# Layer 0 attention in a four-layer kernel: one head at a time, or four heads and blocks of 32 queries

## The reference

```python
q, k, v = heads of (layernorm(x) @ w_qkv.T)          # 16 heads of 8
content = einsum('bhid,bhjd->bhij', q, k)
rel_scores = qE taken at clip(j - i, -64, 64) + 64   # qE = q @ rel_emb.T
scores = (content + rel_scores) / sqrt(8)
scores = where((j > i) | (i - j >= 32), -inf, scores)
out = softmax(scores) @ v
x = x + out @ w_out.T
```

## Time and profile before

| | us |
|---|---|
| median of 3 runs | 3664.6 |
| the profiled execution | 3654.07 |
| its span | 3652.2 |
| stage 3 (preparation of the first attention unit) | 56.0 |
| stage 4 | 100.6 |
| stage 5 | 88.1 |
| stage 6 | 87.3 |
| stage 7 | 113.3 |
| stage 8 (last finish of the attention) | 37.3 |

### The profile page before, as it was taken

How to read it: one execution, slowest core, us unless ns; L and a number is a source line. 1 busy time by engine, 2 the same in 40 slices (tenths; PEclk the granted TensorE clock), 3 DMA queues, 4 the chain that set the end, 5 groups by cost and what they waited for, 6 DMA issues and landing times. The chain is left out here.

```text
span 3652.2 us, 63921 instructions
## 1 busy us (share of the span) xinstructions
PE 2966.9 (81%) x23249; PEld 1869.6 (51%) x23249; DVE 2404.7 (66%) x6402; ACT 1929.6 (53%) x5094; POOL 899.9 (25%) x875
## 2 busy tenths in 40 slices
PE   5868888878987558899787787889887889889875
PEld 3545544544443434456675587656554333556553
DVE  4667765677777456786456543868776677777752
ACT  2356775245553225555246633656664677667652
POOL 1000000011133331111213211635451112444430
PEclk7879988689988779999898988989998899999987
DMA  3423432000000000003660056300000000001010
GB/s 121 166 76 100 110 102 67 1 1 1 1 1 1 1 1 1 1 1 103 222 210 6 12 194 212 100 20 23 14 23 4 1 1 1 21 14 24 13 29 9
DMA packets 132658, 183.41 MB, mean 50 GB/s; under 512 B 48501, under 2 KB 108021, under 8 KB 130682
## 3 DMA queue, kind: packets, MB, share of 16 engines
q1 hardware_dynamic: 129818, 174.14, 15.3%
q0 software_dynamic: 2048, 4.20, 0.3%
q10 hardware_dynamic: 480, 0.98, 0.1%
HBM read 131.90 MB, written 30.61 MB: 44 GB/s over the span
## 5 line engine op out<-in xcount | busy, mean ns | idle before, releaser
L1051 DVE TENSOR_REDUCE nm<-ps 128x1 f32<-128x512 f32 (+4 forms) x832 | 443.3, 564 | 111.8 <-PE ps L972 63.7
L1094 ACT ACTIVATE core<-ps 128x512 f32<-128x512 f32 (+3 forms) x832 | 377.0, 510 | 131.0 <-PE ps L1003 91.7
L274 POOL TENSOR_TENSOR rstd<-ve,weights 128x4 f32<-128x4 f32 x80 | 80.9, 1011 | 1290.4 <-DVE ve L251 1289.9
L969 PE MATMUL ps<-hand 128*128 128x128 bf16 (+3 forms) x1024 | 302.4, 335 | 57.5 <-DVE nm L1051 31.2
L427 ACT COPY hand<-ps 64x512 bf16<-64x512 bf16 x448 | 259.6, 580 | 139.4 <-PE ps L459 100.7
L1000 PE MATMUL ps<-hand 128*128 128x512 bf16 (+3 forms) x1024 | 273.5, 309 | 18.6 <-ACT hand L427 9.4
L1890 POOL TENSOR_TENSOR pre<-pre,sin 128x512 f32<-128x512 f32 x128 | 221.9, 1754 | 241.3 <-ACT pre L1859 225.5
L2006 ACT ACTIVATE core<-ps,nm 128x128 f32<-128x128 f32 x512 | 181.8, 374 | 124.4 <-DVE nm L2021 123.7
L1659 PE MATMUL ps<-hand 128*128 128x128 f32 x1408 | 199.7, 302 | 38.5 <-DMA hand<-in_experts 38.5
L1895 POOL TENSOR_TENSOR ss<-ss,weights 128x16 f32<-128x16 f32 x64 | 194.2, 3035 | 117.4 <-DVE ss L1910 115.9
L1818 PE MATMUL ps<-weights,pre 128*128 128x512 f32 x384 | 207.1, 637 | 17.4 <-ACT pre L1862 17.3
(11 more groups left out here) (331 smaller groups left out, 7542.6 us busy)
## 6 DMA issues: line engine op xcount, KB each, us to landing
hand<-in_experts SPq DMA_DIRECT2D x88, 836.0 KB, 4.9
core<-shear SPq DMA_DIRECT2D x64, 512.0 KB, 3.8
shear<-post SPq DMA_DIRECT2D x64, 256.0 KB
hand<-hand SPq DMA_DIRECT2D x16, 512.0 KB, 4.4
hand<-hand SPq DMA_DIRECT2D x16, 384.0 KB, 5.6
pre<-sorted_in SPq DMA_DIRECT2D x8, 704.0 KB, 4.7
sorted_out<-core SPq DMA_DIRECT2D x88, 64.0 KB, 2.3
core<-in_stream SPq DMA_DIRECT2D x2, 2048.0 KB, 7.8
```

The costliest lines, as they stand in the source:

```text
L969: ins = nc.tensor.matmul(b[:, n * P:n * P + nk], q[:, qt * P:(qt + 1) * P], k[:, lo:lo + nk], start=kind != BLOCK32, stop=True, skip_group ...
L1051: nc.vector.tensor_reduce(nm_of(h, qts), src, AX.X, ALU.max, negate=True).then_inc(negmax, 1)
L1094: nc.scalar.activation(prob8[:, i % PROBS, 0:L - q0], m.ps[:, RING[at % NR], 0:L - q0], ACT.Exp).then_inc(ring_out, 1)
```

## The change

The core is written anew for layer 0; `attend_near` is gone. A unit is now a group of four heads and half of the tokens: 8 units instead of 64. The 512 queries are cut into 16 blocks of 32, each with 64 keys, its own 32 and the 32 before. Four heads lie on the four quarters of the partitions and eight blocks side by side, so a unit's scores are one full bank, 128 x 512. Per unit there are 32 score matmuls (32 columns of weights, 64 moving), three VectorE instructions over 128 x 512 (add, minimum of each 64, subtract), one exp of 128 x 512 without a sum, four transposes, one copy, and 32 fp32 matmuls with the values (64 rows, 32 columns of weights, 32 moving). The row sum comes from a column of ones that already stands in the values, and the division moves to the finish. Half of the blocks have keys that begin at row 32 or 96 of a tile; for them `Vs`, a copy of the values shifted by 32 tokens, is made by two DMAs at the end of the preparation. The relative scores come by 64 DMAs of 32 KB in place of 16 of 512 KB. `far` is a constant that masks the keys before the first block. The finish becomes `divide` (16 transposes, 4 reciprocals, 4 products) and `out_project` (4 transposes, a copy, 4 matmuls, an addition), helpers that other layers use, with a plain output weight of 128 columns where 512 were. The order strings of stages 3 to 8 are new.

```diff
-    [("ip_T", NI), ("pv", 4 * DV), ("l0_qkv", 3 * D), ("l0_out", 4 * D),
+    [("ip_T", NI), ("pv", 4 * DV), ("l0_qkv", 3 * D), ("l0_out", D),
...
-def attend_near(nc, m, note, a, heads, rows_of, value_of, place_of, sheared):
...
+    def vector(dve):
+        yield 0.0
+        dve.wait_ge(*stacks_turned)
+        nc.vector.memset(a.Vs[0:32, 0, :], 0.0).then_inc(none_set, 1)
+
     def sync(sp):
+
+        yield 0.1
+        sp.wait_ge(*stacks_turned)
+        sp.dma_start(a.Vs[32:128, :, :], a.V[0:96, :, :]).then_inc(moved, 16)
+        sp.dma_start(a.Vs[0:32, 1:NT, :], a.V[96:128, 0:NT - 1, :]).then_inc(moved, 16)
...
+    units = [(g, half) for g in range(4) for half in range(2)]
+    U = len(units)
+    BQ, BK = 32, 64
+    NPR, NTS, NREL = 3, 3, 2
+    TURN, WEIGH = 2, 3
+    S, PT, O = (0, 1), (2, 3), (4, 5)
...
+        for t in (2 * half, 2 * half + 1):
+            for odd in range(2):
+                for r in range(2):
+                    yield 4 * t + 2 * r + odd, (t % 2) * 256 + odd * 128 + r * 64, (a.V if odd else a.Vs)[:, t, :], 64 * r
...
+        for g in range(4):
+            yield max(0.0, 2.0 * (g - NREL + 1) + 0.6)
+            if g >= NREL:
+                sp.wait_ge(added, 2 * (g - NREL + 1))
+            for j in range(4):
+                h = 4 * g + j
+                for odd in range(2):
...
+                    for r in range(2):
...
+                        sp.dma_start(dst[:, :, odd, r], src).then_inc(rel_in[g % NREL], 16)
...
+            if i >= 2:
+                pe.wait_ge(added, i - 1)
+            if half == 0:
+                nc.tensor.matmul(out[:, 0:BK], m.identb, m.far, start=True, stop=True)
+            for n, at, _, _ in blocks(half):
+                for j in range(4):
...
+                    ins = nc.tensor.matmul(out[BQ * j:BQ * (j + 1), at:at + BK], q[:, BQ * n:BQ * (n + 1)], keys,
+                                           start=n > 0, stop=True, skip_group_check=True)
...
+            pe.wait_ge(exps, u + 1)
+            if u >= 2:
+                pe.wait_ge(pT_ready, u - 1)
+            for r in range(4):
+                ins = nc.tensor.transpose(m.ps[:, PT[u % 2], r * P:(r + 1) * P], prob[:, u % NPR, r * P:(r + 1) * P],
+                                          m.weight["ident"])
...
+            for n, at, v, row in blocks(half):
+                for j in range(4):
...
+                    ins = nc.tensor.matmul(m.ps[BQ * j:BQ * (j + 1), O[row // BK], to:to + BQ], v[row:row + BK, 9 * h:9 * h + 32],
+                                           pT[row:row + BK, u % NTS, col:col + BQ], start=True, stop=True)
...
+            nc.vector.tensor_tensor(p, bank(m, S[i % 2]), rel[:, g % NREL, half * L:(half + 1) * L], ALU.add).then_inc(added, 1)
...
+            nc.vector.tensor_reduce(lows(i), eight(p), AX.X, ALU.min).then_inc(least, 1)
...
+            nc.vector.tensor_tensor(eight(p), eight(p), lows(i).unsqueeze(2).to_broadcast([P, 8, BK]),
+                                    ALU.subtract).then_inc(shifted, 1)
...
 def l0_attn_post(nc, m, lane, a, b, l):
-    project_turned(nc, m, lane, a.otok, m.weight["l0_out"], m.x[b])
+    divided = divide(nc, m, lane, a.otok, m.post.ot)
+    out_project(nc, m, lane, m.post.ot, m.post.oT, m.weight["l0_out"], None, m.x[b], m.x[b], divided)
```

The new tensor orders of stage 4, of stages 5 and 6, and of stage 7:

```diff
+    {"tensor": "a1c2a1b2a1b2a1b1c1b1a1c1b1a3b2a2b1a1b1c1b1a2b1a3b1a1b1c1b1c1b1a1c1a3c2a2c1",
+    {"tensor": "a2c1b2a1c1b3c1a3b1c1b1c1b1a2b1c1b1a2b1a2b2a3b4a9",
+    {"tensor": "c1a2c1b2a1c1b1a1b1a2b1a2b1a3b1a1c1b1a2b1a3b1c1b1c1a1b1a1b1a1b1a1b1a1b1a1b1a1b2",
```

More of the change, by code:

```diff
@@ L67 @@
 ]
-L0_COLS = NI + 4 * DV + 3 * D + 4 * D
+L0_COLS = NI + 4 * DV + 3 * D + D
 STREAM = [("piw_T", 8 * NP_), ("oiw_T", NI), ("op", 8 * D)]
@@ new lines, in l0_attn_core @@
+    U = len(units)
[3 more added lines that the diff above has]
+    S, PT, O = (0, 1), (2, 3), (4, 5)
+    scores, added, least, shifted, exps, turned, pT_ready, av, o_out = (note(n) for n in (
+        "scores", "added", "least", "shifted", "exps", "turned", "pT_ready", "av", "o_out"))
+    rel_in = [note(f"rel{i}") for i in range(NREL)]
+    prob = m.core[:, 0:NPR * L].rearrange("p (s n) -> p s n", s=NPR)
+    pT = m.core[:, NPR * L:(NPR + NTS) * L].rearrange("p (s n) -> p s n", s=NTS)
@@ new lines, in vector @@
+    def vector(dve):
+        for i in range(U):
+            g, half = units[i]
+            p = prob[:, i % NPR, :]
+            yield i + 0.4
+            dve.wait_ge(scores, i + 1)
+            if half == 0:
+                dve.wait_ge(rel_in[g % NREL], 16 * 16 * (g // NREL + 1))
+            if i >= NPR:
+                dve.wait_ge(turned, i - NPR + 1)
+            nc.vector.tensor_tensor(p, bank(m, S[i % 2]), rel[:, g % NREL, half * L:(half + 1) * L], ALU.add).then_inc(added, 1)
+            yield i + 0.7
+            dve.wait_ge(added, i + 1)
+            nc.vector.tensor_reduce(lows(i), eight(p), AX.X, ALU.min).then_inc(least, 1)
+            yield i + 1.0
+            dve.wait_ge(least, i + 1)
+            nc.vector.tensor_tensor(eight(p), eight(p), lows(i).unsqueeze(2).to_broadcast([P, 8, BK]),
+                                    ALU.subtract).then_inc(shifted, 1)
@@ new lines, in scalar @@
+    def scalar(act):
+        for i in range(U + WEIGH + 1):
+            if i < U:
+                yield i + 1.4
+                act.wait_ge(shifted, i + 1)
+                nc.scalar.activation(prob[:, i % NPR, :], prob[:, i % NPR, :], ACT.Exp, scale=-1.0).then_inc(exps, 1)
+            if TURN <= i < U + TURN:
+                yield i + 1.6
+                u = i - TURN
+                act.wait_ge(turned, u + 1)
+                if u >= NTS:
+                    act.wait_ge(av, u - NTS + 1)
+                nc.scalar.copy(pT[:, u % NTS, :], bank(m, PT[u % 2])).then_inc(pT_ready, 1)
+            if i >= WEIGH and (i - WEIGH) < U and units[i - WEIGH][1] == 1:
+                yield i + 1.8
+                g = units[i - WEIGH][0]
+                act.wait_ge(av, i - WEIGH + 1)
+                own = a.otok[:, g, :].rearrange("p (t r n) -> p r t n", r=2, n=BK)
+                out = m.ps[:, O[0]:O[1] + 1, 0:L // 2].rearrange("p r (t n) -> p r t n", n=BK)
+                nc.scalar.copy(own, out).then_inc(o_out, 1)
@@ L2462, in _ @@
                 nc.vector.memset(m.onesb, 1.0)
+                nc.vector.memset(m.far[:, 0:32], -NEG)
+                nc.vector.memset(m.far[:, 32:64], 0.0)
                 dve.wait_ge(small_in, 16)
```

92 lines of the change are left out of this document (64 added, 28 removed).

## The result

The changed kernel takes 3515.8 us (median of 4 runs, 3510.88 to 3520.95) where the kernel before took 3661.6 beside it (3658.38 to 3666.59): a ratio of 0.960, 95% interval 0.958 to 0.962, so 146 us less.

What follows compares the result with a forecast made beforehand. The core, with no engine free, was taken to bound stages 4 to 7, the preparation below it. Stage savings of 25.6, 16.1, 15.3 and 53.3, +0.5 elsewhere and 6 us allowance gave -104 from 3664.6: 3561 us, range 3525 to 3605.

Steps and rivals of the forecast that it cites:

- The price of a small matmul: Core on TensorE: about 31 ns a step when nothing streams long, each fp32 matmul being two steps.
- W: A unit's 32 fp32 value matmuls on TensorE, 64 steps: 2.1 us, with bounds 1.9 and 3.6.
- Head: Start of stage 5 through unit 2's VectorE work, which needs the second group of 16 score DMAs: 18 us.
- Rival 1: SyncE's DMA issue is dearer, 0.63 us, so stages 4 to 6 end 6 us later: 3581 us; chance 0.12.
- Stack: Stage 5, the preparation's stretch before its eight turns: 6.2 us, taken from the earlier trace.
- Turns: Stage 5, eight preparation turns up to the first relative round: 21.3 us plus 6.4 for core steps and waits.
- Relative rounds: Stage 5, four preparation rounds at 1.3 us, with an exp and a copy ahead of the third: ending at 57.
- Tail: End of stage 5: nine core steps that nothing hides, 13 us, then waits, last copy and border, ending at 72.
- T: A unit's four transposes on TensorE: 0.66 us alone, 0.5 in a row.
- The allowance: Stages 4 to 7: 1.5 us added a stage for uncounted hand-offs and low clock, 6 in all.
- The rest: Finish in stages 5 to 8, stage 3's added DMAs and new strings, +1; smaller load at the start, -0.5.
- Rival 3: The preparation is hardly disturbed, its turns at the full clock and waits hidden: 3527 us; chance 0.08.

Runs made afterwards that it cites:

- wserial: The changed kernel with each unit's value matmuls reordered so that neighbours use the same part of the array, same number: 3536.9 us, ratio 0.966.
- dma32b: The changed kernel with a core's relative scores brought by 32 DMAs of 64 KB instead of 64 of 32 KB: 3493.9 us, ratio 0.956.
- sserial: The changed kernel with each unit's 32 score matmuls issued head by head, so neighbours share a quarter of the columns: 3513.1 us, ratio 0.961.
- old3: The changed kernel with stage 3's order strings from the kernel before, all other stages unchanged: 3511.9 us, ratio 0.960.
- novs: The changed kernel without the two DMAs for the shifted values, the copy filled with ones by VectorE: 3517.3 us, ratio 0.960.

## Why the prediction was right or wrong

**What bounds the kernel** held: the core's many units on all three engines were the limit, and replacing them emptied VectorE and ScalarE. Stages 4 to 7 fell from 389 to 247 us.

**The price of a small matmul failed**, and it is the step that matters: "a step costs about 31 ns when nothing streams long". W was 0.76 to 0.89 us, not 2.1, below even my lower bound of 1.9 ("no less than a step"). The rows from which I took the 31 ns were of matmuls that fill all 128 rows of the array or alternate two halves of the columns; these here go round four quarters of the columns and two halves of the rows. wserial changes only the order: W is back at 1.51 to 2.31 us and the time up by 21 us. Of the 45 us between forecast and result this step is worth 21 by the medians, 15 by the lengths of stages 4 to 7. The Trainium skill, "TensorEngine Tiling (Array Packing)", Instruction Overhead, has some 60 cycles for each matmul; the estimate of 25 ns at 2.4 GHz worked out from it agrees with the 24 ns of wserial's shorter bursts and not with the 12 of the kernel's own order. I weighed 25 against 31 and missed that both could be twice too high. The lower bound was unfounded: no row showed such tiles.

The trace of the kernel before held the hint. Taken one by one, the 16 records of L1994 begin in pairs, 7 ns apart within a pair and, after the first, 58 ns from pair to pair. With wserial in mind I read a pair as two matmuls on the two halves of the columns that ran together, and the 31 ns as their mean, which four quarters could halve again. No run tested this reading of layer 3. And the signs of being wrong that I named were all signs of a slower kernel; none of them came, and the forecast was wrong on the other side.

**Stage 5, term by term.** Forecast 18 + 6.3 + 27.7 + 5 + 15 = 72; measured 21.3 + 6.2 + 20.6 + 4.7 + 10.9 = 63.7.
- *Head*, 3.3 us late. Rival 1 was partly right. The issue was not 0.42 but 0.53 us each in a long row, and the landing shorter than said (1.9, not 2.5). I took it from L1127, whose median of 0.36 us is that of issues which stand alone. In a row the same line says otherwise: of the three that begin at 318.46 the first took 0.36 us and the other two 0.50 each. L2513 at 0.59, to which I gave 0.12, was the closer row. dma32b shows what hangs on the number of issues: 15 us over the kernel by the ratios, 22 by the medians.
- *Stack*, right.
- *Turns*, 7.1 us shorter. I had let W0 S4 and others exceed the gap of a copy, 4.4 us in all, and added two more. (Half a us of the 4.4 was a slip: 3.6 exceeds 1.8 by 1.8, not by 2.3.) With bursts of 0.8 and 0.6 us they fit, and the turns take 20.6, not more than stage 3's 21.3. wserial gives 2.4 of it back, sserial 1.1 (21.7 us). The two us for other engines' steps ahead of copies were not there.
- *Relative rounds*, right.
- *Tail*, 4.1 us shorter. With the durations of the timeline my sum would be five W at 0.89, one S at 0.62, three T at 1.12, then 0.6 for the copy and 1.0 to the border: 10.0 us, where 10.9 were measured with one stand of 1.40 us in them. So here too W was the step, 6.0 us too dear in five bursts; T was 1.9 too cheap, because the granted clock of the stage was 0.59, partly the lower of the two levels, 1.2 GHz. wserial gives back only 1.8; how far the stand hides its dearer bursts I have not tested.

**Stage 4** missed by the same: 67.8 after 75, of which wserial gives back 4.2, on a stage that differs by 2.2 us between profiles.

**Stage 7** was followed rightly as ScalarE's sequence: gelu 7 ended 38.7 us after the start (39.3 forecast), the comparisons began at 41.4 (43). Two terms at its end were too long. I summed mean durations to 1.3 us for a comparison, but the records of VectorE overlap by up to 0.1 us, and the distance from one comparison to the next is 1.06 us:

```profile
455.97 0.29 DVE L691 TENSOR_SCALAR pre<-pre,acc_pre 128x128 bf16<-128x128 f32 x1 [0.55 <-ACT pre L755]
456.17 0.68 DVE L693 TENSOR_SCALAR pre<-pre,acc_pre 128x896 bf16<-128x896 f32 x1
456.77 0.35 DVE L694 SCALAR_TENSOR_TENSOR pre<-pre,acc_pre,weights 128x128 bf16<-128x128 f32 x1
457.03 0.35 DVE L691 TENSOR_SCALAR pre<-pre,acc_pre 128x256 bf16<-128x256 f32 x1
...
458.08 0.42 DVE L691 TENSOR_SCALAR pre<-pre,acc_pre 128x384 bf16<-128x384 f32 x1
```

And W4 to W7, at 0.76 us, pushed the last count by little: border at 52.3, not 60. wserial, with a lower clock in this stage, gives 5.4 of these 7.7 back. It was, as forecast, the stage that gained most, 61 us.

**The allowance** of 1.5 us a stage for a low clock and hand-offs was not needed, though its reason came true: the granted clock fell from 0.88 in stage 4 and 0.94 in 5 and 6 to 0.58, 0.59 and 0.67, while TensorE's busy share of stage 5 fell from 85% to 64%. The copies, for which TensorE now waits in the turns, don't follow that clock: the double copy of a turn takes 1.17 us as before. **The rest** of +0.5 came out near zero, as +2.2 in stage 3 (its strings, old3) and -2.3 in stage 8. The `Vs` DMAs were free (novs).

So of the 45 us: 32 lie in stages 4 to 7 (15 to 21 the price of W, the rest the turns' and the tails' waits and VectorE's overlap, less the slow issue, which went the other way), 6 in the allowance, 1.2 in the rest and the other stages, and 5.6 in the distance from the profiled execution to the median, 10.5 us before and 4.9 now. Rival 3, "hardly disturbed", 3527 us, came closest to the result. Its hidden waits came true in the turns, its full clock did not, and the cheap W it did not name; that its number was near is in good part luck.

## What to carry to other kernels

Price small tiled matmuls by the burst and by whether neighbours share a part of the array, and write the loops so that they don't: here the order of the value matmuls alone was worth 21 us, while the same order on the score matmuls, which lie beside waits, was worth nothing. A lower bound needs a row of the same kind, or it isn't one; and instructions summed by their means come out too long where they overlap, so take distances from the timeline. Where a stage begins with many small DMAs of one engine, count the issues in a row (0.53 us each here for 32 KB; one of 64 KB took 0.45 us where one of 32 KB took 0.43, by the medians), and make them fewer before making them shorter.
